# A two-layer network on one core: a new order in the prologue, in the first steps of attention, and in layer 1

## The reference, cut to what matters

```python
x = L0_attn_X                                  # 4 x 1024 x 128
xn = _layernorm(x)
s = _L0_attn_ref(xn, W_qkv, W_out)             # 16 heads of 64, softmax, no mask
g = _silu(_L0_ffn_ref(xn, router_w, w_fc, w_proj, shared_fc, shared_proj))
x = x + s * g
xn = _layernorm(x)
s = _L1_attn_ref(xn, dt, A, Bmat, C, D, norm_w)
g = _silu(_L1_ffn_ref(xn, w_gate, w_up, w_down))
x = x + s * g
```

## Time and profile before

| | us |
|---|---|
| median of 3 runs | 1996.6 (1996.03 to 1997.16) |
| the profiled execution | 2004.97 |
| its span, first to last instruction | 2003.0 |
| busy: PE, DVE, POOL, ACT | 1838.7, 1519.8, 1421.0, 999.5 |

### The profile page before, as it was taken

The page is one execution under the profiler, slowest core; times in us unless marked ns, Lnnn a source line. Parts: engine busy times, 40 slices in busy tenths (PEclk is TensorE's granted clock), DMA queues, the critical chain, the costliest instruction groups (busy, mean ns, idle before and its releaser), DMA issues. The chain is left out here.

```text
span 2003.0 us, 33228 instructions
## 1 busy us (share of the span) xinstructions
PE 1838.7 (92%) x10419; PEld 1048.3 (52%) x10419; DVE 1519.8 (76%) x2088; ACT 999.5 (50%) x1476; POOL 1421.0 (71%) x852
## 2 busy tenths in 40 slices
PE   4499999999999999999999999999999799965776
PEld 4245555555555555555555555555554588753444
DVE  7467777777777777777777777777777688777765
ACT  1045444445445454454444444454454588754643
POOL 4068888888888888888888888888888166636532
PEclk9999999999999999999999999999999799986989
DMA  6010110101010110101010110101010577230000
GB/s 212 3 54 22 42 54 10 52 10 54 18 53 21 42 54 10 52 10 54 18 52 21 43 52 10 52 10 54 18 52 21 200 242 241 85 85 23 6 11 27
DMA packets 98100, 107.84 MB, mean 54 GB/s; under 512 B 8208, under 2 KB 88016, under 8 KB 94864
## 3 DMA queue, kind: packets, MB, share of 16 engines
q1 hardware_dynamic: 93072, 97.15, 15.0%
q0 software_dynamic: 4992, 10.27, 1.4%
HBM read 52.56 MB, written 26.82 MB: 40 GB/s over the span
## 5 line engine op out<-in xcount | busy, mean ns | idle before, releaser
L1145 POOL TENSOR_TENSOR psum_k<-psum_k,probs 128x1024 f32<-128x1024 f32 x384 | 925.8, 2411 | 199.0 <-ACT probs L1097 184.0
L1162 DVE TENSOR_REDUCE mxh<-ps_m 128x2 f32<-128x1024 f32 x523 | 639.2, 1222 | 266.3 <-PE ps_m L948 264.9
L1097 ACT ACTIVATE probs<-ps_s 128x1024 f32<-128x1024 f32 x512 | 497.3, 1023 | 270.0 <-PE ps_s L965 220.5
L973 PE MATMUL ps_v<-probs,V 128*64 128x512 f32 x2056 | 489.8, 597 | 0.0
L1186 DVE RECIPROCAL rden<-den 128x128 f32<-128x128 f32 x260 | 245.6, 946 | 25.3 <-ACT den L1068 16.2
L973 PEld LDWEIGHTS ps_v<-probs,V 128*64 128x64 f32 x2056 | 137.4, 137 | 235.8 <-issue 232.8
L948 PE MATMUL ps_m<-k_hi,q_hi 64*128 64x512 f32 x1046 | 243.2, 458 | 15.6 <-DVE mxh L1162 11.8
L963 PE MATMUL ps_s<-q_lo,k_hi 64*128 64x512 f32 x1024 | 202.4, 389 | 0.0
L965 PE MATMUL ps_s<-shift,ones_r 64*128 64x512 f32 x1024 | 202.3, 388 | 0.0
L963 PE MATMUL ps_s<-q_hi,k_hi 64*128 64x512 f32 x1024 | 202.0, 390 | 0.0
L963 PE MATMUL ps_s<-q_hi,k_lo 64*128 64x512 f32 x1024 | 202.0, 389 | 0.0
(11 more groups left out here) (274 smaller groups left out, 2815.9 us busy)
## 6 DMA issues: line engine op xcount, KB each, us to landing
e_ew<-w_split SPq DMA_DIRECT2D x23, 1024.0 KB, 6.8
V<-V_next SPq DMA_DIRECT2D x33, 512.0 KB, 3.3
xs_hi<-xh SPq DMA_DIRECT2D x16, 512.0 KB, 3.7
xs_lo<-xl SPq DMA_DIRECT2D x16, 512.0 KB, 4.3
rows<-in_blank_d SPq DMA_DIRECT2D x4, 1483.5 KB, 18.4
e_x_raw<-rows SPq DMA_DIRECT2D x23, 258.0 KB, 3.7
we_raw<-in_experts_d SPq DMA_DIRECT2D x33, 128.0 KB, 2.5
w_split<-we_hi SPq DMA_DIRECT2D x32, 128.0 KB, 1.9
```

What stands on the lines that cost most here:

```text
L973: ins = nc.tensor.matmul(ps_v[rows, :], V[par][:, kt, rows], probs[:, t % RING, x, :], start=kt == 0, stop=kt == KT - 1)
L1097: nc.scalar.activation(probs[:, t % RING, :, :], ps_s[t % 2][:, :, :], ACT.Exp, scale=SCALE).then_inc(p_done, 1)
L1145: nc.gpsimd.tensor_tensor(acc, probs[:, (t - 1) % RING, :, :] if kt == 1 else acc, probs[:, t % RING, :, :], ALU.add).then_inc(add_done, 1)
L1162: nc.vector.tensor_reduce(mxh[:, kh, t, :], ps_m[:, :, :], AX.X, ALU.max).then_inc(m_done, 1)
```

## The change

There are five parts.

1. First stage. Normalising goes to ScalarE, as `x * rstd + nbias`, where GpSimd computes `nbias = -mean * rstd` in two more small products. GpSimd's presets go to the front of its list. The routing chain leaves the stage; `two_largest` ends with the indices, kept in `psum_k[0]`.
2. Presets. Of the ring's eight slots three are set, and these (slot 0, slots 6 and 7) with `psum_k[1]` in the attention block.
3. Start of attention. `FIRST` has another order, its projections take turns in `ps_x` and `ps_v`, the first maxima take turns in `ps_m` and `ps_s[0]`, and the routing chain stands in pieces among them on VectorE; its scratch lies in ring slots 1 and 2.
4. Experts. `weighted` stands at j == 1.
5. Layer 1. ScalarE's list starts each chunk with the sizes of half A, then gates. The state path of the last two batches is divided over chunks, the second scan goes from the end of chunk 2 to the end of chunk 3, the recurrences are read by ScalarE in chunks 2 and 5, and the fourth `hidden` product follows the first steps of half B. The last chunk's transposes, product, gate, rows, copy and store go in two halves, into banks `ps_b` and `ps_c`.

```diff
-            for b in range(B):
+            def normalise(b):
+                act.wait_ge(rstd_done, 3 * b + 3)
+                for t in range(TPB):
+                    x = x_tok[:, b * TPB + t, :]
+                    ins = nc.scalar.activation(x, x, ACT.Identity, scale=rstd[:, b, t:t + 1], bias=nbias[:, b, t:t + 1])
+                ins.then_inc(xn_done, 1)
...
+            normalise(0)
+            normalise(1)
+            high(0)
+            normalise(2)
+            high(1)
+            normalise(3)
+            high(2)
...
-                        if j == 3 and tile(i, s - 3) and not is_routed(*tile(i, s - 3)):
+                        if j == 1 and tile(i, s - 3) and not is_routed(*tile(i, s - 3)):
                             weighted(*tile(i, s - 3))
...
+    def bank(n, name):
+        return ps_v if n is None and FIRST.index(name) % 2 else ps_x
+
+    def max_bank(unit, i):
+        k = unit * KT + i if isinstance(unit, int) else KT + EARLY
+        return ps_s[0] if k < KT + EARLY and k % 2 else ps_m
...
+            nc.gpsimd.memset(ones_n[:, :], 1.0).then_inc(ones_n_done, 1)
+            nc.gpsimd.memset(probs[:, 0, :, :], 0.0).then_inc(preset, 1)
+            nc.gpsimd.memset(probs[:, RING - 2:RING, :, :], 0.0).then_inc(preset, 1)
+            nc.gpsimd.memset(psum_k[1][:, :, :], 1.0).then_inc(add_done, 1)
...
             def body(c):
+                sizes(q_h[0], steps_before(c) + 4)
+                if c == 2:
+                    recurrence(0)
+                if c == 5:
+                    recurrence(1)
+                if c in (1, 3):
+                    normed_T((c + 3) // 2)
                 if not last(c):
                     gates(c + 1, 1)
-                sizes(q_h[0], steps_before(c) + 4)
+                if c in (1, 3):
+                    state_inputs((c + 3) // 2)
...
-                if c == 2:
+                if c == 3:
                     states_of(1)
...
-            hidden_T(LAST)
-            gate(LAST)
+            last_hidden_T(0)
+            last_gate(0)
             finish(LAST - 1)
-            finish(LAST)
+            last_hidden_T(1)
+            last_finish(0)
+            last_gate(1)
+            last_finish(1)
```

More of the change, by code:

```diff
@@ L265, in _ @@
             two_largest(0)
-            normalise(3)
             low(2)
@@ L282, in _ @@
-            step(nc.vector.tensor_scalar(count[:, :], up_to[:, :, TILES - 1], float(CH - 1), None, ALU.add))
-            step(nc.vector.tensor_scalar(count[:, :], count[:, :], CH.bit_length() - 1, None, ALU.logical_shift_right))
-            step(nc.vector.tensor_copy(fills[:, :], count[:, :]))
-            step(nc.vector.tensor_tensor_scan(ends[:, :], ones[:, 0:E], fills[:, :], 0.0, ALU.mult, ALU.add))
-            step(nc.vector.tensor_tensor(starts[:, :], ends[:, :], fills[:, :], ALU.subtract))
@@ L338, in _ @@
             router(3)
-            pe.wait_ge(picks_done, B)
-            pe.wait_ge(mh_done, 2)
-            ones_of = picks[:, :, :].rearrange("p t e -> p (t e)")
-            nc.tensor.matmul(ps_n[0][:, :], before[:, :], ones_of, start=True, stop=True).then_inc(n_ready, 1)
-            nc.tensor.matmul(ps_n[1][:, :], ones[:, :], ones_of, start=True, stop=True).then_inc(n_ready, 1)
 def expert_tiles(nc, ctx, g):
@@ L753, in layer0_attention @@
     at_rows = sb("at_rows", [P, 2, 1], U32)
+    count = sb("count", [P, E], U32)
+    starts = sb("starts", [P, E], F32)
+    ring = [probs[:, k, :, :].rearrange("p x c -> p (x c)") for k in (1, 2)]
+    spare = iter([ring[0][:, k * 256:(k + 1) * 256] for k in range(4)] +
+                 [ring[1][:, a:b] for a, b in ((0, 256), (256, 512), (512, 512 + ROUTED * E), (768, 832), (832, 896),
+                                                           (896, 896 + ROUTED), (928, 960), (960, 968), (968, 976))])
+    pick = [next(spare).rearrange("p (t e) -> p t e", e=E) for k in range(2)]
+    picks = next(spare).rearrange("p (t e) -> p t e", e=E)
+    in_tile = next(spare).rearrange("p (e t) -> p e t", e=E)
+    base = next(spare).rearrange("p (e t) -> p e t", e=E)
+    row = next(spare).rearrange("p (t e) -> p t e", e=E)
+    past = next(spare).rearrange("p (t e) -> p t e", e=E)
+    pos_f = next(spare).rearrange("p (k t) -> p k t", k=2)
+    top_f = next(spare).rearrange("p (t k) -> p t k", k=2)
+    owner = next(spare)
+    total = next(spare)
+    fills = next(spare)
+    ends = next(spare)
+    ones_n = g.ones_n
     ps_s = [pb(f"ps_s{i}", [P, 2, CH]) for i in range(2)]
@@ L919, in max_rows @@
                 for x, rows in enumerate(HEADS):
-                    ins = nc.tensor.matmul(ps_x[rows, 0:P], mxw[:, x, :], g.ident[:, :], start=True, stop=True)
+                    ins = nc.tensor.matmul(bank(n, name)[rows, 0:P], mxw[:, x, :], g.ident[:, :], start=True, stop=True)
                 ins.then_inc(x_ready, 1)
@@ L1205, in add_out, with step, picked_experts @@
                 nc.vector.tensor_tensor(g.sT[:, tok], ps_x[:, :], g.sT[:, tok], ALU.add).then_inc(xv_done, 1)
+            steps = 0
+            def step(ins):
+                nonlocal steps
+                steps += 1
+                ins.then_inc(route, 1)
+                v.wait_ge(route, steps)
+            def picked_experts():
+                wide = [P, TILES, E]
+                step(nc.vector.tensor_copy(top_f[:, :, :], g.top_i[:, :, 0:2]))
+                for k in range(2):
+                    ins = nc.vector.tensor_tensor(pick[k][:, :, :], g.iota8[:, :].unsqueeze(1).to_broadcast(wide),
+                                                  top_f[:, :, k:k + 1].to_broadcast(wide), ALU.is_equal)
+                step(ins)
+                nc.vector.tensor_tensor(picks[:, :, :], pick[0][:, :, :], pick[1][:, :, :], ALU.add).then_inc(picks_done, 1)
@@ L1207, in _, with shares, first_max @@
+            def shares():
+                step(nc.vector.tensor_scalar(total[:, :], g.ratio[:, :], 1.0, None, ALU.add))
+                step(nc.vector.reciprocal(g.weight[:, 0, :], total[:, :]))
+                nc.vector.tensor_tensor(g.weight[:, 1, :], g.weight[:, 0, :], g.ratio[:, :], ALU.mult).then_inc(routed, 1)
+            def first_max(unit, *parts):
+                for i in parts:
+                    row_max(unit, i)
             v.wait_ge(w_in, 64)
             v.wait_ge(preset, PRESETS)
+            picked_experts()
@@ L1219, in _ @@
+            tiles_of_experts()
+            low(None, "K1", 0)
+            first_max(0, 2, 3)
+            first_rows()
+            low(None, "Q1", 0)
+            first_max(0, 4, 5)
+            positions()
+            first_max(0, 6, 7)
+            owners()
+            shifts(None, "max0")
+            first_max(1, *range(EARLY))
+            shares()
             for n, par in pairs(v):
@@ L1823, in body @@
                         quantise_step(nc, k, *stream).then_inc(q_step, 1)
+                    if k == 0 and not last(c):
+                        hidden(c + 1, 3)
                 if c == 0:
                     states_of(0)
-                if c == 2:
+                if c == 3:
                     states_of(1)
```

385 lines of the change are left out of this document (217 added, 168 removed).

## The result

The changed kernel takes **1966.6 us** (median of 4 runs, 1962.9 to 1968.9), the kernel before 1996.3 beside it (4 runs, 1995.6 to 1997.2). The ratio is 0.984, with a 95% interval of 0.9827 to 0.9852: 29.7 us faster. I had forecast 1949 (1938 to 1962), 47.6 us faster. The direction was right, and the time lies 4.6 us above my range.

A forecast was written before the change was run, and what follows sets the result against it. TensorE fills the attention loop, which the change leaves alone; at the edges no engine is full, so waits decide. Gains of 19 + 12 + 5 + 12 = 48 us from the 1996.6 median gave 1949 us, range 1938 to 1962.

The forecast's parts named there:

- The walk: First stage: new order stepped through with old durations; ScalarE normalises from 9.5 us, attention starts at about 47.5 instead of 66.2.
- rival B: Start of attention: the chain of maxima does not overlap, gaining 5 us instead of 12; 1956 us in all; 13%.
- rival D: Loop: entered in another phase, so a pair takes longer and the kernel is slower than before; 2%.
- the 3 us that the prediction worked out by that rule: Experts: differences wait for GpSimd's squares by the port rule, 6.9 us a tile, so the stage gains 3.
- 2004.97 - 48: Whole kernel: the profiled execution's time less the summed gain, giving 1957 us for a profiled execution.
- The walk, 30.6 us of waits replaced by 24.7: Layer 1, body by body: VectorE's 30.6 us of waits at stake return as 24.7 in chunks 0 to 6, gaining 5.9.
- 1.6 us of neighbours that no longer collide: Layer 1: an extra gain of some 1.6 us added to the walk's 5.9, making 7.5.
- The tail, forecast 5.9: Layer 1's end: last chunk in halves, 13.1 us instead of 18.9 from the last split step, 5.9 less.
- 1.4 us that I took off the gain for the clock: Layer 1: new waits in chunks 2 and 3 idle TensorE and may lower its clock; 13.4 us gain cut to 12.
- A: Layer 1 keeps its time as waits return, only tail and 1 us won, experts give 2; 1957 us; 20%.
- C: Everything overlaps: start 14.5, experts 8, layer 1 20, first stage 19, 61 us less; 1935 us; 12%.
- E: The first stage was bound elsewhere (inputs), so the gain is under 20 us in all; 1980 us; 3%.

The follow-up runs named there:

- e11: The changed kernel with all first maxima in one PSUM tile, as before the change; ratio 0.986 to the kernel before.
- e5: The changed kernel, unchanged, run beside its parts on one chip; 1971.8 us, ratio 0.983 to the kernel before.
- e8: The changed kernel with layer 1 as before, except that layer 1's new order is kept (last chunk whole); 1971.0 us, ratio 0.9818 to the kernel before.
- e4: The kernel before with only the experts' change, the weighted sum moved to j == 1; ratio 0.9991 to the kernel before.
- e1: The kernel before, unchanged, profiled a second time on another chip; layer 1 took 202.8 us.
- e6: The changed kernel with layer 1 as before (front and experts changed); 1967.5 us, ratio 0.9806 to the kernel before.
- e7: As e6, but with layer 1's last chunk kept in two halves; 1966.0 us, ratio 0.9792 to the kernel before.
- e17: The kernel of e14 with the second half's gate and transposes earlier and the halves' rows in two PSUM banks; 1956.1 us, ratio 0.9781 to before.
- e14: The changed kernel with the second recurrence behind chunk 5's gates and the last batch's rows scaled earlier in chunk 2; 1957.3 us, ratio 0.9793 to before.

## Why the forecast was right in front and wrong behind

**First stage, forecast 19 us less: 20 to 21.** The walk held in its places: ScalarE began at 9.48 (walk 9.5), attention at 45.5 (walk 47.5; 45.4 to 46.1 in all profiles of the new front). (Its two stalls of 5.8 and 3.2 us make 9.0, not 9.5; no term hangs on it.)

**Start of attention, forecast 12 us less: 12 to 14 as a rule.** 28.2 to 29.8 us in twelve of fifteen profiles, 26.4 in three, the first profile of the changed kernel among them; the last section shows that TensorE reached its faster pace earlier in these three, worth some 3 us here. The 7 us that I priced for rival B are what e11 gave back.

**Loop, forecast unchanged: unchanged.** 1442.4 to 1444.4 us; rival D did not show.

**Experts, forecast 5 us less: 1.5, between two profiles.** The stage scatters by more than that (240.7 to 246.2 us in e5 to e8, with the same code on one chip), and e4's median is 2 us lower and not told from nothing; so the size is open, but not the step that failed: the sum over removed waits. They went: TensorE waited 11.6 us for the sum and waits 5.7 now. But the work that took their place on VectorE grew. Timelines of VectorE, one tile, and of GpSimd beside it, in the changed kernel:

```profile
1723.30 1.11 DVE L623 SCALAR_TENSOR_TENSOR x_tok<-e_y,weight,e_ps_y 128x128 f32<-128x128 f32 x4
1724.44 1.93 DVE L623 SCALAR_TENSOR_TENSOR x_tok<-e_y,weight,x_tok 128x128 f32<-128x128 f32 x4
1726.29 4.18 DVE L610 TENSOR_TENSOR e_h_lo<-e_relu,e_h_hi 128x512 fp32r<-128x512 f32 x4
...
1723.18 1.09 POOL L578 TENSOR_TENSOR e_relu<-e_relu 128x512 f32<-128x512 f32 x1 [0.36 <-ACT e_relu L513]
1724.59 1.11 POOL L578 TENSOR_TENSOR e_relu<-e_relu 128x512 f32<-128x512 f32 x1 [0.31 <-ACT e_relu L513]
```

The four operations of the second row take 1.14 us in the kernel before, and the sums now come every 7.09 us instead of 7.76: 3.7 us over the first four, of which the last ones gave back 2.4. The form that reads PSUM beside one SBUF tile stayed at 1.11 us, with a square at 1723.18 beside it; the one that reads two SBUF tiles went from 1.14 to 1.93 with the square at 1724.59 beside it. The Trainium skill's page "SBUF — State Buffer" (section "SBUF: two separate sides") draws that line, between VectorE operations with one and with two SBUF inputs against a GpSimd operation that reads SBUF; the trace agrees, and the 3 us that the prediction worked out by that rule were nearer than its 5.

**Layer 1, forecast 12 us less: 2 to 4 us more.** Here some 15 of the missing 18 us lie, and four terms failed.

- The base, "2004.97 - 48" with waits of 25.2 us. I took 209.6 us and 25.2 us of waits for sizes from one execution. Five of nine profiles with the old order do not have its long chunk 4; e1 and e6 show 202.8 and 202.5 us, and waits for sizes of 21.0 and 20.8. e1's execution took the median of its chip (2010.8 and 2010.6); that the median of 1996.6 also holds the shorter kind is likely by this, but none of the executions behind it was profiled. I had noted that the profiled execution lay 8.4 us over the median, and treated the 8.4 as lying outside my terms.
- The walk, 30.6 us of waits replaced by 24.7. Against its own base it was nearly right: all waits of VectorE in chunks 0 to 6 are 38.0 us in the first profile of before and 33.9 in the changed kernel, 4.1 less where I had 5.9. But in e6 they are 32.6 us, and nothing is left. Inside, chunk 2 waits 9.3 us where the walk had 5.7, and chunk 5 6.6 where it had 2.6: gates behind sizes and recurrence make hidden tiles late, 6.4 us of waits in e6 and 17.2 now, and I priced too little of it.
- The "1.6 us of neighbours that no longer collide", for which I had no row. VectorE's busy time in the stage rose instead, from 144.1 us (e6) to 146.7; 1.3 of it is the longer scan. Together: in the groups of waits above, VectorE waits 20.8 + 10.6 + 6.4 + 7.8 = 45.6 us in e6 and 17.8 + 17.2 + 4.3 + 3.7 + 3.6 + 2.2 = 48.8 in the changed kernel, 3.2 more; it works 2.6 us longer; behind its last product the end comes 2.4 us sooner. The stage is 3.4 us longer.
- The tail, forecast 5.9: 0.4 between e6 and e7. 13.1 us assumed that the second half queues behind nothing. Product of chunk 6 and split half, 2.6 us in the sum, take 4.1 with the 1.70 us wait, and the transposes come 3.3 us after the scaling. e17, where little stands ahead of the second half, takes 13.6.

The 1.4 us that I took off the gain for the clock can't be told apart here: the mean granted clock of the stage is 0.83 in e6 and in the changed kernel.

**Rivals.** A (layer 1 keeps its time, 20%) was the nearest in mechanism, and still 10 us too low, since it too started from the long execution. B, C, D and E did not happen. By my own test, "not shorter than 205 us", the layer 1 term had failed at 205.9.

**What stays open.** Front 0.9815, layer 1 1.001 and experts 0.9991 would add to 0.9816; the whole gives 0.983 to 0.984, 3 to 5 us more. The layer 1 change costs 2 us alone and 4 behind the new front. Added up, the intervals of the parts overlap that of the whole, so this may be scatter; I have no row for a difference.

## What to carry to other kernels

Before subtracting from a median, take a second profile of the kernel before and compare the stages: a surplus of the profiled execution can sit in one stage (here layer 1 was 6.8 us longer than in e1), and the waits read there may be of a kind that most executions lack. When a step is moved ahead in an engine's queue, list what every engine waits for from that queue, not only the wait that the move was made for: here the recurrence behind the sizes cost two engines 6 us of taking turns, and moving it back behind the gates, with one 2.4 us step, made the change's order worth having (e14: 1957.3 us, against 1966.1 for the changed order and 1962.2 for the old one, on one chip). When a piece is split in two, look at what stands ahead of the second half in each queue: here the split won 0.4 us in the profiles, and 1.7 more with the second half's steps ahead. And compare chunk with chunk only at the same clock: two kernels' profiles of one chunk differed by 2 to 3.4 us with no other difference than a low stretch.
